# Probabilities, hop outputs and normalised rows of a graph attention kernel placed at 0 modulo 128 bytes

## What is computed

```python
# layer A
q, k, v = x @ Wq.T + bq, x @ Wk.T + bk, x @ Wv.T + bv        # split in 8 heads
pros = softmax(where(adj == 0, -16384, q @ k.T))
z = v
for _ in range(4): z = 0.9 * (pros @ z) + 0.1 * v            # four hops
x = layernorm(x + z) * gamma + beta
# layer B
nx = layernorm(x) * ln1_g + ln1_b
attn = softmax(q @ k.T / sqrt(32) + where(adj > 0, 0.1 * adj * adj, -inf))   # q, k, v from nx
x1 = x + (attn @ v) @ wo + bo
out = x1 + gelu(layernorm(x1) @ w1 + b1) @ w2 + b2           # w1 256x1024, w2 1024x256
```

## Time and profile before

| | |
|---|---|
| median of 3 runs | 2246.26 us (2245.17 to 2248.73) |
| the profiled execution: its time | 2243.45 us |
| its span, first to last instruction | 2241.6 us |
| mean granted TensorE clock | 0.996 of full |
| PE busy (share of the span) | 2211.5 us (99%) |
| PEld | 2120.6 us (95%) |
| DVE | 1836.9 us (82%) |
| ACT | 1934.4 us (86%) |
| POOL | 1544.8 us (69%) |
| DMA queues, share of 16 engines | 10.5% and less |

### The profile page before, as it was taken

How to read it: one execution, slowest core, us unless ns; L and a number is a source line. 1 busy time by engine, 2 the same in 40 slices (tenths; PEclk the granted TensorE clock), 3 DMA queues, 4 the chain that set the end, 5 groups by cost and what they waited for, 6 DMA issues and landing times. The chain is left out here.

```text
span 2241.6 us, 78295 instructions
## 1 busy us (share of the span) xinstructions
PE 2211.5 (99%) x29492; PEld 2120.6 (95%) x29492; DVE 1836.9 (82%) x6993; ACT 1934.4 (86%) x6478; POOL 1544.8 (69%) x1613
## 2 busy tenths in 40 slices
PE   7999999999999999999999999999999999999998
PEld 6999999999999999999999999999999999999988
DVE  5888888888888888888888888888888888877885
ACT  6788988988888889889889888888898898888876
POOL 6776767766776777676677677767776776766752
PEclk8999999999999999999999999999999999999999
DMA  4101011011011011010110110110110101101000
GB/s 133 33 30 33 23 33 40 28 33 39 21 40 40 21 40 35 26 40 28 33 40 28 33 40 21 39 40 21 40 34 27 40 28 33 40 28 40 26 11 18
DMA packets 95781, 76.88 MB, mean 34 GB/s; under 512 B 9648, under 2 KB 95152, under 8 KB 95408
## 3 DMA queue, kind: packets, MB, share of 16 engines
q1 hardware_dynamic: 93632, 71.73, 10.5%
q10 hardware_dynamic: 1776, 0.14, 0.1%
HBM read 55.06 MB, written 16.78 MB: 32 GB/s over the span
## 5 line engine op out<-in xcount | busy, mean ns | idle before, releaser
L881 POOL TENSOR_TENSOR probs<-probs,rinv 128x512 f32<-128x512 f32 x512 | 562.3, 1119 | 363.6 <-DVE rinv L737 363.6
L599 ACT ACTIVATE probs<-probs,negmax 128x128 f32<-128x128 f32 x2048 | 794.6, 394 | 7.8 <-DVE negmax L723 4.0
L599 ACT ACTIVATION_READ_ACCUMULATOR probs<-probs,negmax 128x1 f32 x2048 | 394.1, 192 | 0.0
L809 DVE TENSOR_TENSOR hT_low<-hidden,hT_high 128x512 fp32r<-128x512 f32 x256 | 267.7, 1047 | 42.0 <-ACT hT_high L640 41.9
L533 PE MATMUL ring_ps<-w_high,hT_high 128*128 128x256 f32 x1024 | 294.4, 288 | 1.2 <-DVE hT_low L809 1.2
L395 PE MATMUL ring_ps<-inT_C_high,w_high 128*128 128x256 f32 x1024 | 289.6, 283 | 0.6 <-DVE inT_C_low L694 0.6
L533 PE MATMUL ring_ps<-w_low,hT_high 128*128 128x256 f32 x1024 | 283.5, 277 | 0.0
L533 PE MATMUL ring_ps<-w_high,hT_low 128*128 128x256 f32 x1024 | 283.4, 277 | 0.0
L395 PE MATMUL ring_ps<-inT_C_low,w_high 128*128 128x256 f32 x1024 | 283.3, 277 | 0.0
L395 PE MATMUL ring_ps<-inT_C_high,w_low 128*128 128x256 f32 x1024 | 283.1, 276 | 0.0
L469 PE MATMUL ring_ps<-ident,probs 128*128 128x128 f32 x2048 | 269.6, 276 | 0.2
(11 more groups left out here) (150 smaller groups left out, 7085.2 us busy)
## 6 DMA issues: line engine op xcount, KB each, us to landing
xT_sb<-in_xT_dram SPq DMA_DIRECT2D x64, 256.0 KB, 2.8
x_sb<-in_x_dram SPq DMA_DIRECT2D x64, 256.0 KB, 3.1
out_dram<-x SPq DMA_DIRECT2D x128, 128.0 KB, 1.8
adj_B<-in_adj_dram SPq DMA_DIRECT2D x64, 128.0 KB, 2.2
adj_A<-in_adj_dram SPq DMA_DIRECT2D x64, 128.0 KB, 2.5
probsT_B<-in_L_gnn_w_dram SPq DMA_DIRECT2D x1, 1024.0 KB, 8.6
qT_B<-in_L_gnn_Wq_dram SPq DMA_DIRECT2D x1, 256.0 KB, 4.7
kT_B<-in_L_gnn_Wk_dram SPq DMA_DIRECT2D x1, 256.0 KB, 5.1
```

Source lines behind the costliest of these rows:

```text
L599: e = act.activation(probs[:, u, h, :], probs[:, u, h, :], ACT.Exp, bias=negmax[:, u, h:h + 1], scale=-1.0, accum_out=sums[:, u, h:h + 1])
L809: dve.tensor_tensor(hT[1][:, 2 * f:2 * f + 2, :], hidden[:, f % 2, :, :], hT[0][:, 2 * f:2 * f + 2, :], ALU.subtract).then_inc(s_h_low, 1)
L881: pool.tensor_tensor(probs[:, u, hs, :], probs[:, u, hs, :], rinv[:, u, hs].unsqueeze(2).to_broadcast([P, HR, P]), ALU.mult).then_inc(s_pr ...
```

## The change

Three declarations move up, ahead of `hT`; nothing else in the program differs, and every later line number grows by one where it lies behind them all. Each engine has the same instructions in the same order.

```diff
@@ -215,6 +215,10 @@
         w1_p = parts("w1", [P, C, FF])
 
         oT = parts("oT", [P, GB, C, P])
+
+        probs = sb("probs", [P, 2 * GB, NH, P])
+        zT = [sb(f"zT{k}", [P, GB, C, P]) for k in range(HOPS)]
+        nx, n2 = sb("nx", [P, GB, H]), sb("n2", [P, GB, H])
         hT = parts("hT", [P, FC, T])
 
@@ -246,14 +250,11 @@
         z = [sb(f"z{k}", [P, GB, H]) for k in range(HOPS - 1)]
         y = sb("y", [P, GB, H])
         x1 = sb("x1", [P, GB, H])
-        probs = sb("probs", [P, 2 * GB, NH, P])
         negmax = sb("negmax", [P, 2 * GB, NH])
         sums, scaled, rinv = (sb(n, [P, 2 * GB, NH]) for n in ("sums", "scaled", "rinv"))
         probsT_A = [sb(f"probsT_A{i}", [P, GB, NH, P]) for i in range(2)]
         probsT_B = sb("probsT_B", [P, GB, NH, P])
-        zT = [sb(f"zT{k}", [P, GB, C, P]) for k in range(HOPS)]
         x1b = sb("x1b", [P, GB, H])
-        nx, n2 = sb("nx", [P, GB, H]), sb("n2", [P, GB, H])
```

## The result

The changed kernel takes **2263.63 us** in the median (2262.04 to 2264.54), against 2247.06 us for the kernel before in the same series: ratio **1.0076** (95% interval 1.0064 to 1.0089), 16.6 us slower. The forecast was 2246.3 us, with a range up to 2254.0. The profiled execution took 2263.12 us, with a span of 2261.3 us, 19.7 us more than before.

The account below looks back on a forecast made before the run. TensorE, at work in 99% of the span, was taken to set the time by how closely matmuls follow one another. Five terms summed to 0 us, giving 2246.3 us for the median, range 2237.0 to 2254.0.

Parts of the forecast that it names:

- Term 1: Hidden loads of the 3584 transposes, start moved from 64 to 0 modulo 128: 0 ns taken, bounds -9.0 and +14.7 us.
- cover: At the transposes: a load costs about 60 ns, hidden behind a 109 ns matmul with some 49 ns to spare.
- Terms 2, 3 and 5: Unhidden transpose loads, writers and rewriters of the moved tensors, and set-up: 0 each, with -2 us for the loads in the range.
- term 4: Everything that only shifts by a multiple of 128 (hT, biases, ident, inT, qT, turned probabilities): 0.
- The slower rival: Transpose's tile load and ident's stream hold each other up: 4.1 ns on each of 3584, +14.7 us, 2261.0 us; chance 0.14.
- The closing paragraph: Transposes unchanged but time moved over 4.5 us: products by parts beside busy probs writers, or ScalarE's and GpSimd's probs work.

Follow-up runs that it names:

- the far place: Early SBUF place of probs, zT, nx and n2 as in the changed kernel; with all at 64 modulo 256 there, ratio 1.0001 to the kernel before.
- the kernels of the table: Kernels with turned tiles, ident or inT_C shifted by fillers, other matmul operands kept modulo 256, against the kernel before: ratios 0.9989 to 1.0076.
- the first series: Changed kernel with fillers: all four tensors at 64 modulo 128, or zT, probs, or nx and n2 alone at 0: 1.0022, 1.0000, 1.0072, 1.0081.

## Why the prediction was wrong

**What bounds the kernel: right.** TensorE is at 99% and its 19.8 us more of busy time are the whole difference of the spans; no other engine, and no wait, took part.

**Term 1, the loads of the transposes: right in itself.** 0 ns was taken, and the distance of the transposes is what it was (2.24 us for twenty); the loads of `probs` take 141 ns after as before. Group of PEld after, to be held against the earlier trace rows:

```profile
L470 PEld LDWEIGHTS ring_ps<-ident,probs 128*128 128x128 f32 x2048 | 224.3, 141 | 25.9 <-issue 24.2 <-POOL probs L882 0.7
```

That their loads are hidden fits this; how much cover they have, 49 ns by the prediction, no run tests. Terms 2, 3 and 5 were right too: the pauses of the load queue before these loads sum to 25.9 us (26.1), the set-up wait is 7.7 us (7.8), ScalarE's copy into `zT` at 0 takes 594 ns (595 at 64), exp 394 ns, GpSimd's product 1118 ns (1119).

```profile
L621 ACT ACTIVATE zT<-ring_ps 128x512 f32<-128x512 f32 x256 | 152.0, 594 | 110.8 <-PE ring_ps L478 110.6
```

**The step that failed is term 4, "everything that only shifts by a multiple of 128: 0", together with the picture behind term 1 that moving a transpose's tile can cost time only at the transpose itself.** The products by parts were put at nothing because their instructions and their places modulo 128 stay. Their own shifts did cost nothing (1.0001 with the turned tiles at 64 in the far place); what had no term is that they run behind moved tiles. They took the whole loss: about 380 ns a turn, all of it in the two runs behind `zT`. A run of products has two distances it can keep, and which one it gets hangs on the places of tile and identity in the transposes ahead, and on what the run before that did. The rows for this stood in the trace of before: a tenth of the distances was 117 ns or more in a kernel whose typical one is 113.3, and I read the 1.02 us of nine products and the 1.25 us of eleven as *the* distance of a product, without asking when it is another.

**The slower rival had nearly the size (+14.7 us for 16.6) by the wrong mechanism, which is luck.** It took the 4.1 ns from the difference between a product and a transpose and put them on 3584 transposes. The real price is some 4 ns, on some 4900 products (96 in each of 51 turns), and no transpose pays it. What the rival had right is that the places of tile and identity both count: moving either can take the loss away. That it is how far apart they lie, 96 before and 32 after, is refuted: with the tiles at 64 and the identity 32 behind them again the ratio is 1.0000. What was missing is a rival in which the products pay; and the range left the upper half of the slower case out on the ground that the transposes had 49 ns of cover, which is beside the point.

**The closing paragraph named it.** "If the transposes keep their distance and the time still moves", it said, the products would be it; the cause it gave, busy writers of `probs`, is refuted by `probs` alone at 128 (1.0002) and by `zT` alone (1.0044 with `probs` where it was before).

**What stays open** is what the two states are inside the chip. Shown is that the same places modulo 256 give the same times, that the two distances differ by 10 cycles a product, that in the kernels of the table most runs that are at 117.5 ns from their start began with a second distance of 200 to 202 ns in place of 205 to 207 (many that begin so fall back), and that what one run does reaches the next over a step of transposes. That a load and a stream lock into one of two orders would fit; no run here looks into it. Places alone do not settle it turn by turn: in the kernel before `wB_q` keeps 117.5 ns in 6 turns and 113.3 in 45. What else differs from turn to turn, the PSUM bank or the buffer of a pair for one, was not tried. Nor was a rule found that gives the state from the places: the table has to be measured.

## What to carry to other kernels

Where TensorE is at 99%, print the distance between the starts of two matmuls as a distribution, not as a mean, and run by run: a second value at 4% more is a state that some layouts fall into in nearly every turn and others in few. A change of SBUF places is a change for every matmul in the stream, those that touch no moved tensor included, so compare all places modulo 256, add fillers in pairs that keep the rest of the layout, and try moving the one small shared operand first: 64 bytes ahead of the identity gave back 0.8% here, though the same move did nothing in the kernel before (1.0001). A layout that is "aligned" by some rule isn't better for it; of the eighteen measured here the kernel before is within 0.11% of the best.

## What the runs showed of the hardware that was not expected

- A place modulo 256 bytes counts for TensorE, not only modulo 128: tiles at 0 and tiles at 128 of 256 differ by half a per cent of the kernel's time (1.0026 and 1.0076), and a move of the tiles by whole 256s, 94976 bytes for `probs`, changes nothing that can be told (1.0001).
- A run of 128x128 by 256 products in fp32r keeps 113.3 or some 117.5 ns for up to 70 products, through changes of both operands (in the first series, with other places, it changes at `wB_v`). In one kernel and one layout the same run can keep 113.3 ns in one turn and 117.5 in another (6 of 51 before).
- Stationary and moving operand both at 128 modulo 256 gave 120 ns, only as long as that pair lasted. The Trainium skill (SBUF — State Buffer, Who interferes with whom) gives TensorE two independent read ports, one for each operand, and says that it never waits on anyone. The 120 ns show 6.7 ns more a product for this pair than for either place alone with 64; that it is the two reads that meet is an argument, which no run here shows. That no other engine holds TensorE up agrees with the trace as far as it goes: with `probs`, on which VectorE, ScalarE and GpSimd all work, alone at 128 the time is the same (1.0002).
